# A DLRM forward pass on one core: straight-line gathers with a buffer per tile, and top and dense layers over up to four tiles

## The reference

```python
FIELDS, VOCAB, BATCH, D = 26, 12500, 2048, 64
emb   = emb_tables[arange(26)[:, None], x_cat]        # 26 x 2048 rows of 64 f32
dense = price[:, None] @ Wp + bp                      # 2048 x 64
feats = concat([emb.transpose(1, 0, 2), dense[:, None, :]], axis=1)   # 2048 x 27 x 64
gram  = einsum('bid,bjd->bij', feats, feats)
inter = gram[:, iu, ju]                               # 351 pairs above the diagonal
h     = relu(dense @ W1 + b1)                         # 64 -> 128
d_out = relu(h @ W2 + b2)                             # 128 -> 64
t     = relu(concat([inter, d_out], axis=1) @ Wt1 + bt1)   # 415 -> 256
out   = (t @ Wt2 + bt2)[:, 0]                         # 2048
```

## Time and profile before

| | |
|---|---|
| device time, median of 3 runs | 771.14 us (768.77 to 771.28) |
| span of the profiled execution, first to last instruction | 540.9 us |
| own time of the profiled execution beyond its span | not recorded apart |
| POOL busy | 393.8 us, 73% |
| PE busy | 291.1 us, 54% |
| ACT busy | 246.8 us, 46% |
| DVE busy | 190.2 us, 35% |
| gathers | 416, mean 944 ns |

### The profile page before, as it was taken

The page is one execution under the profiler, slowest core; times in us unless marked ns, Lnnn a source line. Parts: engine busy times, 40 slices in busy tenths (PEclk is TensorE's granted clock), DMA queues, the critical chain, the costliest instruction groups (busy, mean ns, idle before and its releaser), DMA issues.

```text
span 540.9 us, 6578 instructions
## 1 busy us (share of the span) xinstructions
PE 291.1 (54%) x1932; PEld 234.6 (43%) x1932; DVE 190.2 (35%) x672; ACT 246.8 (46%) x816; POOL 393.8 (73%) x425
## 2 busy tenths in 40 slices
PE   0027465382744638466382644727275372786785
PEld 0017354271533517255271533616154261574564
DVE  3016043160613416053160612516043160612553
ACT  0127255271734527265281733637255281733653
POOL 6777777777777777777777777777777777777750
PEclk9997758576585856667567685767758586588888
DMA  6333332333333333333333333333332333332110
GB/s 186 27 26 30 25 27 26 27 26 26 26 27 26 27 26 27 25 26 26 26 27 26 27 27 25 27 26 27 26 26 26 27 26 26 26 26 26 29 23 1
DMA packets 14345, 16.07 MB, mean 30 GB/s; under 512 B 7169, under 2 KB 7425, under 8 KB 14209
## 3 DMA queue, kind: packets, MB, share of 16 engines
q0 software_dynamic: 13312, 13.66, 31.2%
q1 hardware_dynamic: 578, 2.19, 1.1%
q10 hardware_dynamic: 448, 0.14, 0.1%
HBM read 15.95 MB, written 0.01 MB: 29 GB/s over the span
## 4 chain that ended last, share of the span: by engine, by line
POOL 70%; issue 26%; PE 1%; ACT 1%; DMA 1%; POOLq 1%; DVE 0%
POOL gathered L191 70%; PE ps_mlp L432 1%; ACT gram L129 1%; DMA gathered<-in_table,tile_idx 1%; DMA raw_idx<-in_x_cat 0%; POOLq L185 0%; PE ps_gram L414 0%; POOLq L40 0%; POOLq L189 0%; PE ps_mlp L425 0%; PE ps_mlp L440 0%; DVE feats L154 0%; DVE top L336 0%; ACT scores L249 0%; PE ps_trans L383 0%
## 5 line engine op out<-in xcount | busy, mean ns | idle before, releaser
L191 POOL DMA_INDIRECT gathered<-in_table,tile_idx x416 | 392.7, 944 | 128.6 <-issue 126.5
L383 PE MATMUL ps_trans<-ident,gathered 128*128 128x128 f32 x208 | 50.1, 370 | 189.9 <-DMA gathered<-in_table,tile_idx 189.0
L129 ACT COPY gram<-ps_gram 32x56 f32<-32x56 f32 x512 | 131.1, 256 | 41.9 <-PE ps_gram L414 35.2
L129 DVE COPY gram<-ps_gram 32x56 f32<-32x56 f32 x512 | 130.1, 254 | 54.4 <-PE ps_gram L414 46.6
L414 PE MATMUL ps_gram<-feats 64*128 64x128 f32 x1024 | 112.8, 395 | 38.1 <-ACT feats L139 18.2
L414 PEld LDWEIGHTS ps_gram<-feats 64*128 64x128 f32 x1024 | 102.4, 295 | 49.2 <-DVE gram L129 25.5
L139 DVE COPY feats<-ps_trans 64x256 f32<-64x256 f32 (+1 forms) x120 | 45.3, 378 | 218.4 <-PE ps_trans L383 217.2
L383 PEld LDWEIGHTS ps_trans<-ident,gathered 128*128 128x128 f32 x208 | 30.5, 180 | 205.8 <-issue 148.3
L219 ACT CAST tile_idx<-row_idx 128x8 uint32 (+3 forms) x61 | 12.0, 196 | 203.3 <-PE ps_trans L383 202.7
L432 PE MATMUL ps_mlp<-gram,wt1p_sb 128*128 128x128 f32 x448 | 69.6, 317 | 18.1 <-ACT gram L129 14.9
L432 PEld LDWEIGHTS ps_mlp<-gram,wt1p_sb 128*128 128x128 f32 x448 | 63.4, 225 | 24.1 <-DVE gram L129 21.5
(11 more groups left out here) (26 smaller groups left out, 56.6 us busy)
## 6 DMA issues: line engine op xcount, KB each, us to landing
gathered<-in_table,tile_idx POOLq DMA_INDIRECT x416, 3.3
price_bc<-in_price SPq DMA_DIRECT2D x1, 1024.0 KB, 5.7
wt1p_sb<-in_wt_pairs SPq DMA_DIRECT2D x1, 896.0 KB, 8.3
raw_idx<-in_x_cat SPq DMA_DIRECT2D x1, 195.0 KB, 3.2
w_sb<-in_w ACTq DMA_DIRECT2D x2, 32.0 KB, 5.4
wt1d_sb<-in_wt_dense ACTq DMA_DIRECT2D x1, 64.0 KB, 8.2
consts_sb<-in_consts ACTq DMA_DIRECT2D x1, 4.5 KB, 2.0
raw_idx<-in_x_cat SPq DMA_DIRECT2D x1, 13.0 KB, 1.8
```

Source lines behind the costliest of these rows:

```text
L129: last = copy(gram_to[QUAD * c:QUAD * (c + 1), :, RG * r:RG * (r + 1), :, s], gram_from[r % 2][QUAD * s:QUAD * (s + 1), :, :, s, 0:SLABS, c])
L191: pool.indirect_dma_start(out=gathered[:, f * D:(f + 1) * D], out_offset=None, in_=rows, in_offset=bass.IndirectOffsetOnAxis(ap=tile_idx[: ...
L383: last = nc.tensor.transpose(ps_trans[c % 2][:, k * P:(k + 1) * P], gathered[:, f * D:(f + 2) * D], ident[:, :])
```

## The change

Each tile gets its own part of `gathered` (`BUFFERS = TILES`), and POOL reads the index columns straight from `row_idx`, which is now uint32, so `tile_idx` and ACT's copies into it are gone. POOL's loop is written out: 15 tiles of two chunks (14 and 12 fields), then the last tile in the four old chunks. Ahead of a chunk POOL waits only until the same chunk of the tile before has landed. A tile's gram takes two rounds of 16 matmuls into one set of four PSUM banks, and each of DVE and ACT empties a round with 8 copies of twice the size. Dense layers, top layer and score run once per batch of tiles (`BATCHES`: three of four tiles, one of two, two of one), in the first tile of the next batch. The last tile keeps its four rounds and its warming matmuls; those of the tile before it are gone. PE, ACT and DVE are written out without loops.

The core of the diff:

```diff
-ROUNDS = 4
+ROUNDS = 2
 RG = GROUPS // ROUNDS
 SLABS = -(-SLOTS // GROUP)
 BANK = 512
-CHUNKS = [(0, 8), (8, 16), (16, 24), (24, 26)]
-
-
-WARM = {TILES - 2: (0, 12, 4, 1, 1), TILES - 1: (0, 7, 3, 1, 1)}
+CHUNKS = [(0, 14), (14, 26)]
+NC = len(CHUNKS)
+
+LAST = TILES - 1
+LAST_CHUNKS = [(0, 8), (8, 16), (16, 24), (24, 26)]
+LAST_ROUNDS = 4
+LAST_RG = GROUPS // LAST_ROUNDS
+
+BATCHES = [(0, 4), (4, 8), (8, 12), (12, 14), (14, 15), (15, 16)]
+WIDE = 4
+BUFFERS = TILES
+
+WARM = (0, 7, 3, 1, 1)
 TO_GRAM, TO_TOP = 4, 5
 NPAIR = SLOTS * (SLOTS - 1) // 2
+ROW = FIELDS * D
...
                                base=0, pattern=[[-1, P]], channel_multiplier=1).then_inc(ident_made, 1)
-            with pool.Fori(0, TILES) as t:
+
+            def gather(t, f, done):
+                at, to = t * FIELDS + f, (t % BUFFERS) * FIELDS + f
+                pool.indirect_dma_start(out=gathered[:, to * D:(to + 1) * D], out_offset=None, in_=rows,
+                                        in_offset=bass.IndirectOffsetOnAxis(ap=row_idx[:, at:at + 1], axis=0))\
+                    .then_inc(done, 16)
+
+            for t in range(LAST):
+                if t == 0:
+                    pool.wait_ge(rows_made, 1)
+                else:
+                    pool.wait_ge(rows_made, 3)
                 for c, (f0, f1) in enumerate(CHUNKS):
-
-                    pool.wait_ge(tile_idx_set[c], t + 1)
-                    pool.nop(nofuse=True)
+                    if t > 0:
+                        pool.wait_ge(chunk_gathered[c], 16 * (f1 - f0) * t)
                     for f in range(f0, f1):
-                        pool.indirect_dma_start(out=gathered[:, f * D:(f + 1) * D], out_offset=None, in_=rows,
-                                                in_offset=bass.IndirectOffsetOnAxis(ap=tile_idx[:, f:f + 1], axis=0))\
-                            .then_inc(chunk_gathered[c], 16)
+                        gather(t, f, chunk_gathered[c])
+
+            for c, (f0, f1) in enumerate(LAST_CHUNKS):
+                for f in range(f0, f1):
+                    gather(LAST, f, last_gathered[c])
...
+            def gram_round(t, r):
+                wait_trans_evac(NC * (t + 1))
+                pe.wait_ge(dense_slot_set, 2 * (t + 1))
+                wait_gram_evac(ROUNDS * t + r)
+                gram_matmuls(RG * r, RG, 0, 2 * BANK).then_inc(gram_done, 1)
+
+            def gram_last(r):
+                if r == LAST_ROUNDS // 2:
+
+                    wait_trans_evac(NC * LAST + len(LAST_CHUNKS) - 1)
+                    keep_warm(TO_GRAM, 0)
+                wait_trans_evac(NC * LAST + (2 if r < LAST_ROUNDS // 2 else len(LAST_CHUNKS)))
+                pe.wait_ge(dense_slot_set, 2 * TILES)
+                wait_gram_evac(ROUNDS * LAST + max(r - 1, 0))
+                gram_matmuls(LAST_RG * r, LAST_RG, 2 * BANK * (r % 2), BANK).then_inc(gram_done, 1)
+
+            def top_layer(n):
+                w = width(n)
                 for m in range(2):
+                    pe.wait_ge(dense_out_made, n + 1)
+                    nc.tensor.matmul(ps_mlp[m][:, 0:w], wt1d_sb[:, m * P:(m + 1) * P], dense_out[:, 0:w],
+                                     start=True, stop=False)
                     if m == 0:
-                        pe.wait_ge(dense_out_made, t + 1)
-                    else:
-
-                        pe.wait_ge(score_stored, t + 1)
-                    nc.tensor.matmul(ps_top[m], wt1d_sb[:, m * P:(m + 1) * P], dense_out[:, :], start=True, stop=False)
-                    if m == 0:
-                        keep_warm(t, TO_TOP, 1)
-
-                        pe.wait_ge(gram_evac_dve, ROUNDS * t + ROUNDS + 2)
-                        pe.wait_ge(gram_evac_act, ROUNDS * t + ROUNDS + 2)
+                        if BATCHES[n][1] == TILES:
+                            keep_warm(TO_TOP, 1)
+                        wait_gram_evac(ROUNDS * BATCHES[n][1] + (LAST_ROUNDS - ROUNDS if BATCHES[n][1] == TILES else 0))
                     for j in range(SLABS):
-                        last = nc.tensor.matmul(ps_top[m], wt1p_sb[:, j * TM1 + m * P:j * TM1 + (m + 1) * P],
-                                                gram[:, j * P:(j + 1) * P], start=False, stop=(j == SLABS - 1))
+                        at = ((n % 2) * SLABS + j) * WIDE * P
+                        last = nc.tensor.matmul(ps_mlp[m][:, 0:w], wt1p_sb[:, j * TM1 + m * P:j * TM1 + (m + 1) * P],
+                                                gram[:, at:at + w], start=False, stop=(j == SLABS - 1))
                     last.then_inc(top_summed[m], 1)
 
-            def score(t):
-
...
+            for t in range(LAST):
+                n = batch_of[t]
+                first = t == BATCHES[n][0]
+                transpose_chunk(t, 0)
+                if first and n > 0:
+                    top_layer(n - 1)
                 transpose_chunk(t, 1)
-                if not first:
-                    score(t - 1)
-                hidden_layer(t)
-                transpose_chunk(t, 2)
-                dense_out_layer(t)
-                transpose_chunk(t, 3)
-                gram_rounds(t, range(ROUNDS), NC)
-
-                transpose_chunk(t + 1, 0)
```

More of the change, by code:

```diff
@@ L266, in _ @@
-            odd_fields(0, 0)
-            tile(0, first=True)
-            with act.Fori(1, TILES - 2) as t:
-                tile(t)
-            tile(TILES - 2, next_evacuate=evacuate_unit_chunk)
-            t = TILES - 1
-            dense_parts(t)
-            odd_fields(1, t, False, evacuate_unit_chunk)
-            hidden_relu(t)
-            dense_out_relu(t)
-            store_scores(t - 1)
-            for r in range(ROUNDS // 2):
+                evacuate_gram(nc.scalar.copy, t, r, (2, 3)).then_inc(gram_evac_act, 1)
@@ L342, in tile, with top_relu @@
+            def top_relu(n):
+                dve.wait_ge(top_summed[1], n + 1)
+                nc.vector.tensor_scalar(top[1][:, 0:width(n)], ps_mlp[1][:, 0:width(n)], const(BT1 + 1), 0.0,
+                                        ALU.add, ALU.max).then_inc(top_made, 1)
+            for t in range(LAST):
+                n = batch_of[t]
+                even_fields(0, t)
+                if t == BATCHES[n][0] and n > 0:
+                    top_relu(n - 1)
+                even_fields(1, t)
                 for r in range(ROUNDS):
@@ L343, in tile @@
                     gram_round(r, t)
[L344 to L354 removed]
+            t, n = LAST, batch_of[LAST]
+            even_last(0)
+            top_relu(n - 1)
+            even_last(1)
@@ new lines, in dense_out_layer, with gram_matmuls @@
+            def dense_out_layer(n):
+                pe.wait_ge(hidden_made, n + 1)
+                nc.tensor.matmul(ps_mlp[1][0:BM2, 0:width(n)], w2_sb[:, :], hidden[:, 0:width(n)], start=True, stop=True)\
+                    .then_inc(dense_out_summed, 1)
+            def gram_matmuls(first, groups, to, apart):
+                for g in range(groups):
+                    for h in range(2):
+                        at = (first + g) * GROUP
+                        group = feats[D * h:D * (h + 1), at:at + GROUP, :].rearrange("p s j -> p (s j)")
+                        out_at = to + h * apart + g * P
+                        last = nc.tensor.matmul(ps_gram[:, out_at:out_at + P], group, group, start=True, stop=True)
+                return last
@@ L473, in _ @@
-            score(t)
+            for t in range(LAST):
+                n = batch_of[t]
+                first = t == BATCHES[n][0]
+                transpose_chunk(t, 0)
+                if first and n > 0:
+                    top_layer(n - 1)
+                transpose_chunk(t, 1)
+                if first and n > 0:
+                    score(n - 1)
+                gram_round(t, 0)
+                if first:
+                    hidden_layer(n)
+                gram_round(t, 1)
+                if first:
+                    dense_out_layer(n)
@@ L476, in pair_places @@
+            n = batch_of[LAST]
+            transpose_last(0)
+            top_layer(n - 1)
+            transpose_last(1)
+            score(n - 1)
+            hidden_layer(n)
+            dense_out_layer(n)
+            for r in range(LAST_ROUNDS // 2):
+                gram_last(r)
+            transpose_last(2)
+            transpose_last(3)
+            for r in range(LAST_ROUNDS // 2, LAST_ROUNDS):
+                gram_last(r)
+            top_layer(n)
+            score(n)
 def pair_places():
```

302 lines of the change are left out of this document (138 added, 164 removed).

## The result

The changed kernel takes 872.24 us (870.84 to 874.74, 4 runs) against 769.95 for the kernel before: ratio 1.1335, interval 1.1308 to 1.1362. The forecast was 771.1, no change. It was wrong by 101 us: where none was forecast, there is a loss of 13%.

A forecast was written before the change was run, and what follows sets the result against it. POOL's 416 gathers were taken to bound the kernel: 5.71 + 516.76 + 18.4 = 540.9 us of span. All changes summed to 0; with 230.2 us carried over, 771.1 us, range 766.5 to 776, no change at 0.70.

The forecast's parts named there:

- so I make the sum on 540.9 and carry 230.2 over as a constant: Whole run: 540.9 us is the profiled span; the other 230.2 us of 771.14 were put outside it, unchanged.
- GpSimd is held in runs without the profiler: Rival, faster: the 230.2 us are holds at 64 chunk starts, 3.6 us each, which the change removes; chance 0.04.
- These are all hidden as long as POOL is never asked to wait: Steady tiles: gram copies and wide top layers stay behind POOL's gathers, 32.4 us a tile; cost 0.
- POOL's pace: 416 gathers on POOL, 1.248 us apart: 0.944 us instruction and 0.30 us gap; the last starts near 522.5.
- first two steps: POOL's own gathers and gaps bound the kernel, at 1.248 us each; another pace or an idle piece over 0.3 us disproves them.
- neither VectorE's nor ScalarE's activity shows in POOL's pace: Gathers on POOL: shortest and median differ by 4 ns, so the other engines' activity was taken not to affect them.
- Waits for landings, nops, first indices: Landing waits on POOL have 10.7 and 13.2 us spare, 64 nops go, one 26-wide add replaces four; each charged 0.
- Code loading: Rival, slower: POOL's straight run of 416 gathers stalls two to four times, 1.8 us each, 775 to 778 us; chance 0.07.
- turns of the loop: Rival, faster: 15 turns of POOL's loop hid 0.30 us each, 4.5 us, giving 766.6 us; taken 0, chance 0.05.
- Serial rounds of tile 14: Rival, slower: PE and copies between 493 and 509 us run late, end moves by up to 6 us, 777; chance 0.05.
- clock in the tail: Last tile's work on PE: between -1.6 us if never slow and +3.0 us if slow all along; taken 0.
- Top layers over four tiles: Wide top layer on PE, 19.3 us per four tiles, may delay a second chunk by up to 9.5 us; hidden, charged 0.

The follow-up runs named there:

- e4: The kernel before, unchanged, traced again on chip C beside the changed kernel: 765.4 us, with a span of 763.6 us.
- e7: The changed kernel with one wait per tile added on POOL, until ACT has emptied the last gram round two tiles back: 716.8 us, before 771.7.
- e8: The kernel before, all engines written out, with a gather buffer per tile and POOL waiting only for the previous tile's landing: 867.7 us, before 771.7.
- e2: The kernel before with POOL's loop alone written out, waits and nops kept, on chip A: 544.2 us, before 543.7.
- e1: The kernel before with PE, ACT and DVE written out without loops, POOL's loop kept, on chip A: 543.7 us, before 543.7.
- e6: The kernel before with PE, ACT and DVE written out without loops, POOL's loop kept, on chip C: 738.4 us, before 763.7.
- e16: The changed kernel with a 128x1024 memset on POOL after every fourth gather, timed: 623.8 us, 0.8175 of before.
- e17: The kernel before with POOL written out and a 128x1024 memset after every fourth gather, none of the rest of the change: 639.0 us, 0.8364 of before.
- e14: The changed kernel with a 128x8 memset on POOL after each gather: 828.9 us, before 764.7.

## Why the prediction was wrong, point by point

- **The step that failed**, in its words: "so I make the sum on 540.9 and carry 230.2 over as a constant". The 230 us lay within the span: in e4, 205.6 us of it are POOL's hold. The sum has no term for signals that come late. I had the hold as the rival at 0.04 and argued from a trace where it stood 17.7 us away; a page whose span is 30% under the run's time isn't a page of those runs.
- **The rival "GpSimd is held in runs without the profiler" had the fact right and the sign wrong.** The hold is real, with the profiler too, and the change freed POOL, 168.1 us; but the rival took as given that PE keeps up. "These are all hidden as long as POOL is never asked to wait" is the second step that failed: PE was served at one instruction per 1.25 to 1.40 us for as long as POOL was never asked to wait, 64 to a round, so a round took 80 us and more, where a tile's gathers take 32.4. e7 and e8 show it from both sides.
- **POOL's pace**: 1.250 us from gather to gather up to the 174th, as forecast (1.248), then mostly 1.40, and nine idle pieces are over 0.3 us, up to 0.9, so the last gather was at 558.2 and not 522.5. By the prediction's own sign both count against its first two steps; what slows POOL there isn't shown. The step "neither VectorE's nor ScalarE's activity shows in POOL's pace" asked what shows in POOL's pace, and not whether POOL's gathers show in PE's.
- **Waits for landings, nops, first indices**: 0, as forecast; no idle piece on POOL is put down to another engine or a landing but the first.
- **Code loading, turns of the loop**: 0 on chip A (e2: 544.2 against 543.7). The Trainium skill's rule on straight code ("Runtime: NRT & Kernel Launch", Instruction fetch mechanics) shows no gain of its own at POOL there; for PE, ACT and DVE it shows none on chip A (e1: 543.7) and, whatever the cause, 25 us on chip C (e6). The launch figure of the Trainium skill ("Runtime: NRT & Kernel Launch", The ~15µs preamble/postamble breakdown), about 9 to 15 us, spoke for what I gave 0.04: it left 215 us to explain. The measurement is smaller still, since 1.8 to 2.2 us of each execution lie outside its span here. The rule should have weighed more than my constant.
- **Serial rounds of tile 14, clock in the tail**: not tested by after's end, since PE was far behind; a copy of 112 elements took 3.05 / 8 = 0.38 us, above my 0.30 and within the bounds of 0.256 and 0.512. Where PE keeps up the end is near the forecast's 17 to 21 us: e16 ends 622.1 - 601.98 = 20.1 us after its last gather.
- **Top layers over four tiles**: charged 0. Their price is not shown by itself; the whole change beside the memsets gains 15 us (e16 against e17).

## What to carry to other kernels

When the traced execution and the timed ones differ by more than the 2 us seen here, find out first which of the two the change will meet; a constant hides a mechanism. On six of the seven chips A to G, back-to-back indirect gathers hold up PE's signals, so a wait that idles GpSimd may be what lets PE work: before removing it, ask what else stands still when it is gone. A memset of 1 us on GpSimd after every fourth gather costs POOL some 44 us (last gather at 602.0, where after has 558.2) and brought the changed kernel from 872 to 624 us.

## What the runs showed of the hardware that I had not expected

- Beside indirect gathers 0.30 us apart, PE's instructions are signalled at one per 1.25 to 1.40 us, 64 or so started ahead of that; beside plain loads by POOL or SP, or gathers 2.08 us apart, a round of 64 is signalled in 3.8 us. By what path gathers do this no run shows; DVE's signal at 124.57 wasn't late, POOL's own was in e14. Every execution of the experiments has a span and so was recorded by the profiler; whether the recording has a part in the late signals is not tested.
- It was so on six chips and not on one, where only before and its variants e1 and e2 were run; the time of the kernel before differs by 40% between them.
